# Score matmuls of 128 keys issued as four matmuls of 32 keys, one to each column group of TensorE

## The chip, the cores and the metric

The kernel runs on one core of one Trainium2 chip. The metric is the device time of one execution in microseconds (us). Work is spread over TensorE (PE in the profile; PEld is its weight loading), VectorE (DVE), ScalarE (ACT), GpSimd (POOL) and the DMA queues that SyncE (SP) issues.

## The reference

The reference embeds 1,024 patch tokens and 77 text tokens for each of 8 batches (1,101 tokens of 64 features), adds a state-space layer, and then adds this attention block, which takes about two thirds of the time:

```python
sx = jnp.einsum('bsh,ndh->bnsd', x, hl_w) + hl_b[None, :, None, :]
q = jnp.einsum('bnsd,neod->bneso', sx, wq)          # 4 heads n, 4 experts e, 16 features
k = jnp.einsum('bnsd,nod->bnso', sx, wk)            # one key set per head, shared by its experts
v = jnp.einsum('bnsd,nod->bnso', sx, wv)
scores = jnp.einsum('bnesd,bntd->bnest', q, k) * d ** 0.5 + causal
att = jax.nn.softmax(scores, axis=-1)
qkv = jnp.einsum('bnest,bntd->bnesd', att, v)
...                                                 # gate over experts, layer norm, two 16x16 layers, gate over heads
```

So for each batch, head and expert there are 1,101 queries by 1,101 keys under a causal mask.

## The kernel before, in words

The program has three parts: the embedding with the state-space layer, `stage_ffn_bounded` (the attention, on which everything below bears), and `stage_ffn_exact`, a second form of the attention behind a flag that these inputs do not set.

In `stage_ffn_bounded` the tokens are padded to 9 tiles of 128. Queries `qop` and keys `kop` lie in SBUF as 97 rows (six bf16 part products of 16 features and one row for a bound) by tokens. A **score matmul** (`scores`, L1923 to L1936) loads 128 keys of 97 rows as weights and streams up to 512 queries of one expert past them; in the last query tile, of 77 queries, one matmul streams the 77 queries of all four experts, 308 columns. Its result, 128 keys by queries, fills a PSUM bank of `pss`. `score_units` packs the pieces in banks and two banks in a unit: 23 units a head and 57 score matmuls a head (24 of 512 columns, 8 each of 384, 128 and 256, and 9 of 308). ScalarE takes the exponential of a unit (`b_pb<-b_pss`, L2051), GpSimd masks the diagonal blocks (L2089), and then the **value matmuls** (`sums`, L1938 to L1960) multiply the 32 columns of `vop` with the exponentials. The value matmul of expert e writes partitions 32e to 32e+31 of `pso`, so four of them, one per expert, stand in four column groups of the array. They are issued for 13 groups a head, each of one or two units, sorted so that the four experts of a key tile follow each other.

One batch is a period of 92 slots (4 heads of 23 units). In slot s TensorE issues the score matmuls of unit s, then, where a group is complete, the value matmuls of the units two slots back, then the **fillers** that the tables `PRO`, `EPI`, `ATT` and `RES` put in this slot: the projections of the next batch (L1918, L1995, L1998, L2003, L2007, L2010, L2011), the mixer of the finished head (L1986) and the layers behind the attention of the batch before (L1918, L2015, L2020). TensorE takes them strictly in this order. `scores` waits until the exponential two units back has been taken (`exped`), in the first unit of a head until the head's operands have landed (`placed`); `sums` waits for `exped` and `masked`.

`periods` (L1819) runs a first half period without attention, one period written out for batch 0, a loop whose body is run six times for batches 1 to 6, and two more written out. At the end of a body TensorE jumps back to its start. In slots 50 to 76 VectorE splits the next batch's queries and keys into bf16 parts (L2191 to L2196); SyncE stores them to DRAM (L1856 to L1867) and loads them back, head by head, in the layout of `qop` and `kop` (L1873, L1874, and the bound at L1878). The first unit of the next batch waits for head 0 of that.

Of the kernel before, what the change touches and what calls it, by code (L numbers as in the profile page):

```python
# [14 lines left out]
P = 128  # L15
# [78 lines left out]
NH, NE, HD = 4, 4, 16  # L94
# [1007 lines left out]
VW = 32  # L1102
# [578 lines left out]
def stage_ffn_bounded(nc, w, h2d, out, flag_d):  # L1681
# [15 lines left out]
    with ExitStack() as ctx:  # L1697
# [18 lines left out]
        qop = sb("b_qop", [KB_, NH, NE, LP], BF16)  # L1716
        kop = sb("b_kop", [KB_, NH, LP], BF16)
# [26 lines left out]
        pss = ps("b_pss", [P, 2, UB, QT])  # L1744
# [86 lines left out]
        with nc.Block() as block:  # L1831
# [69 lines left out]
            def _(pe):  # L1901
# [21 lines left out]
                def scores(p, u):  # L1923

                    n, un = divmod(u, NU)
                    if un == 0:
                        pe.wait_ge(placed[n], (p + 1) * (13 * 16))
                    pe.wait_ge(exped, p * NUB + u + 1)
                    for b, bank in enumerate(units[un]):
                        for col, j, e, q0, w in bank:  # L1930
                            lhs = kop[:, n, j * P:(j + 1) * P]
                            if e is None:
                                mm = pe.matmul(pss[:, u % 2, b, 0:NE * w], lhs, qop[:, n, :, q0:q0 + w], start=True, stop=True, skip_group_check=True)  # L1933
                            else:
                                mm = pe.matmul(pss[:, u % 2, b, col:col + w], lhs, qop[:, n, e, q0:q0 + w], start=True, stop=True, skip_group_check=True)  # L1935
                    mm.then_inc(scored, 1)  # L1936

                def sums(p, u):  # L1938
# [84 lines left out]
                def run(p, att, pro, prev):  # L2023
                    k[0], first[0] = 0, parity(p)
                    at = jobs(att, pro, prev)
                    if att and not prev:
                        pe.wait_ge(late_ok, 5)
                    for s in range(SPAN):
                        if att:
                            scores(p, s)  # L2030

                        if s < LAG and prev:
                            sums(p - 1, SPAN - LAG + s)
                        elif s >= LAG and att:
                            sums(p, s - LAG)
                        for kind, c in at.get(s, ()):
                            fill(jobs_before(p), p, kind, c)
# [423 lines left out]
```

## Time and profile before

| | |
|---|---|
| Median of 3 runs | 1675.55 us (1671.19 to 1684.4) |
| Profiled execution, span | 1670.1 us (the profile gives no other time for it) |
| TensorE matmul busy | 1341.6 us, 80% of the span, 11,103 matmul records |
| TensorE weight load busy | 628.3 us, 11,103 records |
| VectorE, ScalarE, GpSimd busy | 881.8, 775.4, 419.2 us |
| Mean granted TensorE clock | 0.845 of 2.4 GHz |

How to read it: times in the rows are microseconds from the start of the span, unless they are marked ns or are the mean of one instruction, which is in ns. An fp32 matmul of the program leaves two load records and two matmul records, a bf16 one leaves one of each. The record of a matmul covers its whole passage; the next may start long before its end, so what a matmul costs in a stream is the step from start to start. "issue" is time in which the engine waited for nothing that the profile shows.

### The profile page before, as it was taken

To read this page: it belongs to the slowest core of one execution; us is meant where nothing else is said; L and a number is where in the kernel's file an instruction comes from. 1 tells how busy PE (TensorE), PEld (TensorE's weight loads), DVE (VectorE), ACT (ScalarE), POOL (GpSimd) and SP (SyncE) were. 2 spreads that over 40 slices of the span, in tenths; PEclk is the share of its full clock that TensorE was granted. 3 is DMA by queue.
4 is the path that set the end of the run, shared out by engine and by line. 5 is a ranking of instruction groups with operands and counts; after the bars stand their busy time and mean duration, and the time that the engine had idled before them with its cause. 6 is when DMAs were issued, how large, how long until landed. Compare 5 with 4: busy or idle time off the path is not lost.

```text
span 1670.1 us, 32129 instructions
## 1 busy us (share of the span) xinstructions
PE 1341.6 (80%) x11103; PEld 628.3 (38%) x11103; DVE 881.8 (53%) x1824; ACT 775.4 (46%) x906; POOL 419.2 (25%) x619
## 2 busy tenths in 40 slices
PE   5888388915499899978988997899789979998942
PEld 3454287712154334323433432343234334333421
DVE  4667833275545544744673464538345735852343
ACT  0231244310256564556555455645564655675730
POOL 2000400053122241323323132423133232323421
PEclk9998699655599987889997888979797989998975
DMA  8995698031630360063036004500720270072000
GB/s 149 186 239 78 121 196 162 1 80 23 124 49 12 81 100 1 12 128 62 12 79 110 1 12 104 85 1 12 143 46 12 66 123 1 12 140 41 2 14 8
DMA packets 121421, 118.09 MB, mean 71 GB/s; under 512 B 73848, under 2 KB 90503, under 8 KB 121109
## 3 DMA queue, kind: packets, MB, share of 16 engines
q1 hardware_dynamic: 117216, 115.41, 36.1%
q8 instruction: 98, 1.61, 0.5%
q10 hardware_dynamic: 3733, 0.60, 0.3%
q14 instruction: 54, 0.44, 0.1%
q0 software_dynamic: 320, 0.04, 0.0%
HBM read 88.17 MB, written 22.95 MB: 67 GB/s over the span
## 4 chain that ended last, share of the span: by engine, by line
PE 41%; DVE 15%; issue 7%; DMA 5%; POOL 4%; SPq 3%; ACT 2%; DVEq 0%; POOLq 0%; ACTq 0%
PE b_pso L1959 13%; PE b_pss L1935 12%; POOL b_stat L2070 3%; PE b_psm L1986 3%; DMA qk_parts_b<-b_qs 3%; PE b_psm L2015 3%; ACT b_pb L2051 2%; PE b_psm L2003 2%; DMA b_qop<-bound_part 2%; PE b_psm L1918 2%; DVE b_rq L2193 2%; PE b_psm L1998 2%; PE b_psm L1995 1%; DVE b_qs L2191 1%; PE b_psm L2020 1%
## 5 line engine op out<-in xcount | busy, mean ns | idle before, releaser
L2051 ACT ACTIVATE b_pb<-b_pss 128x1024 f32<-128x1024 f32 (+2 forms) x736 | 667.7, 937 | 559.8 <-PE b_pss L1935 459.2
L2089 POOL TENSOR_SCALAR_AFFINE_SELECT b_pb<-b_pb 128x256 f32<-128x256 f32 (+1 forms) x544 | 230.4, 441 | 822.8 <-ACT b_pb L2051 816.8
L1959 PE MATMUL b_pso<-b_pb,b_vop 128*32 128x77 f32 (+4 forms) x5376 | 405.3, 414 | 27.1 <-POOL b_pb L2089 25.3
L1935 PE MATMUL b_pss<-b_qop,b_kop 97*128 97x512 bf16 (+3 forms) x1536 | 368.9, 357 | 67.7 <-issue 59.4
L1935 PEld LDWEIGHTS b_pss<-b_qop,b_kop 97*128 97x128 bf16 x1536 | 125.7, 106 | 295.2 <-issue 137.7
L1959 PEld LDWEIGHTS b_pso<-b_pb,b_vop 128*32 128x32 f32 x5376 | 118.2, 117 | 220.7 <-issue 138.4
L2278 DVE TENSOR_TENSOR b_ofm<-b_pso,b_mk 128x512 f32<-128x512 f32 (+1 forms) x96 | 51.6, 538 | 199.6 <-PE b_pso L1959 196.8
L2070 POOL TENSOR_TENSOR b_stat<-b_stat,b_mh 128x18 f32<-128x18 f32 x34 | 108.9, 3220 | 38.8 <-DVE b_stat L2349 27.3
L915 PE MATMUL psc<-tz,ub 128*64 128x128 f32 x1152 | 79.9, 283 | 44.7 <-DVE tz L1036 36.1
L2156 DVE COPY b_ot<-b_psm 128x336 f32<-128x336 f32 (+1 forms) x96 | 40.2, 418 | 133.9 <-PE b_psm L1986 132.8
L1986 PEld LDWEIGHTS b_psm<-w_mixer,b_ofm 128*128 128x128 f32 (+1 forms) x576 | 74.9, 200 | 75.2 <-issue 52.8
L1986 PE MATMUL b_psm<-w_mixer,b_ofm 128*128 128x84 f32 (+1 forms) x576 | 90.8, 298 | 1.1 <-DVE b_ofm L2278 0.3
L915 PEld LDWEIGHTS psc<-tz,ub 128*64 128x64 f32 x1152 | 71.8, 141 | 52.6 <-DVE ub L1032 33.7
L2003 PE MATMUL b_psm<-b_xt,w_all 65*128 65x384 f32 (+1 forms) x144 | 71.0, 584 | 11.3 <-DVE b_rq L2193 11.0
L396 PE MATMUL psy<-x,g 128*128 128x512 f32 x128 | 64.3, 660 | 8.5 <-DMA x<-in_x 5.3
L1933 PE MATMUL b_pss<-b_qop,b_kop 97*128 97x308 bf16 x288 | 64.1, 305 | 0.0
L1036 DVE COPY tz<-tz 64x1152 f32<-64x1152 f32 x40 | 29.7, 753 | 46.5 <-DMA tz<-taps 46.3
L956 ACT COPY tz<-tz 64x1152 f32<-64x1152 f32 x24 | 27.6, 1151 | 57.2 <-DMA tz<-taps 57.2
L1007 POOL TENSOR_TENSOR stat<-stat,mh 128x18 f32<-128x18 f32 x4 | 16.1, 4033 | 132.8 <-DVE stat L1066 132.8
L1918 PE MATMUL b_psm<-w_ident,b_xn 128*64 128x128 f32 x72 | 12.8, 293 | 43.3 <-DVE b_xn L2321 43.3
L396 PEld LDWEIGHTS psy<-x,g 128*128 128x128 f32 x128 | 26.4, 213 | 39.8 <-issue 30.8
L997 POOL MEMSET mh<- 128x18 f32 x1 | 0.1, 118 | 161.0 <-POOLq L252 161.0
(378 smaller groups left out, 1539.1 us busy)
## 6 DMA issues: line engine op xcount, KB each, us to landing
b_qop<-qk_parts_b SPq DMA_DIRECT2D x192, 144.0 KB
tz<-taps SPq DMA_DIRECT2D x64, 304.0 KB, 9.6
x<-in_x SPq DMA_DIRECT2D x16, 1024.0 KB, 13.5
qk_parts_b<-b_qs SPq DMA_DIRECT2D x16, 864.0 KB, 5.2
b_kop<-qk_parts_b SPq DMA_DIRECT2D x192, 36.0 KB
b_mk<-b_mskf SPq DMA_DIRECT2D x128, 36.0 KB, 4.1
qk_parts_b<-b_ks SPq DMA_DIRECT2D x8, 432.0 KB, 3.9
n_late<-id_d SPq DMA_DIRECT2D x1, 2400.0 KB, 9.4
```

Source lines behind the costliest of these rows:

```text
L396: mm = pe.matmul(psy[:, j, :], g[:, r], x[:, b % 3, 8 * j:8 * j + 8, r * V:(r + 1) * V], start=(r == 0), stop=(r == KB - 1))
L915: pe.matmul(psc[D * half:D * half + D, g, c, :], ub[:, g, c, o:o + D], taps_at(dl), start=(dl in (0, 2)), stop=(dl == 7), skip_group_check ...
L1933: mm = pe.matmul(pss[:, u % 2, b, 0:NE * w], lhs, qop[:, n, :, q0:q0 + w], start=True, stop=True, skip_group_check=True)
L1935: mm = pe.matmul(pss[:, u % 2, b, col:col + w], lhs, qop[:, n, e, q0:q0 + w], start=True, stop=True, skip_group_check=True)
L1959: mm = pe.matmul(pso[VW * ee:VW * (ee + 1), (3 * n + x) % 2, q0 - QT * x:q0 - QT * x + w], vop[0:r, j, n, :], pb[0:r, slot_, b, cc:cc + w] ...
L1986: mm = pe.matmul(bank()[0:wd, (a - c[0]) * MIXW:(a - c[0] + 1) * MIXW], ofm[:, (3 * n + x) % 2, (a - c[0]) * P:(a - c[0]) * P + wd], mixer ...
L2003: mm = pe.matmul(bank()[0:m, 0:FB], wall[:, g * P:g * P + m], xt[:, x * FB:(x + 1) * FB], start=True, stop=True)
L2015: mm = pe.matmul(bank()[0:D, 0:FB], fcw[:, i, :], (hx1 if i else fxt)[:, c * FB:(c + 1) * FB], start=True, stop=True)
L2051: nc.scalar.activation(pb[:, s % PB, 0:nb, 0:w], pss[:, s % 2, 0:nb, 0:w], ACT.Exp, scale=float(HD) ** 0.5).then_inc(exped, 1)
L2070: pool.tensor_tensor(st[:, 3, lo:hi], st[:, 2, lo:hi], mh[:, lo:hi], ALU.pow).then_inc(rstd, 1)
L2089: ins = pool.affine_select(out=v_, in_=v_, compare_op=ALU.is_ge, fill=0.0, base=0, pattern=pat, channel_multiplier=-1)
L2278: tt(ofm[:, (3 * n + x) % 2, 0:w], pso[:, (3 * n + x) % 2, 0:w], mk[:, n, QT * x:QT * x + w], ALU.mult).then_inc(acc_free, 1)
```

## The change

Each score matmul is replaced by four, whose weights are 32 of the 128 keys and whose results go to the 32 matching partitions of the same columns of `pss`. Each of the four streams the same queries. What is computed, the banks, the semaphores and the order of units, value matmuls and fillers stay. `VW` is 32 and `P` is 128. The exact form behind the flag is not changed.

```diff
                     for b, bank in enumerate(units[un]):
                         for col, j, e, q0, w in bank:
-                            lhs = kop[:, n, j * P:(j + 1) * P]
-                            if e is None:
-                                mm = pe.matmul(pss[:, u % 2, b, 0:NE * w], lhs, qop[:, n, :, q0:q0 + w], start=True, stop=True, skip_group_check=True)
-                            else:
-                                mm = pe.matmul(pss[:, u % 2, b, col:col + w], lhs, qop[:, n, e, q0:q0 + w], start=True, stop=True, skip_group_check=True)
+                            for g in range(P // VW):
+                                lhs = kop[:, n, j * P + VW * g:j * P + VW * g + VW]
+                                if e is None:
+                                    mm = pe.matmul(pss[VW * g:VW * g + VW, u % 2, b, 0:NE * w], lhs, qop[:, n, :, q0:q0 + w], start=True, stop=True, skip_group_check=True)
+                                else:
+                                    mm = pe.matmul(pss[VW * g:VW * g + VW, u % 2, b, col:col + w], lhs, qop[:, n, e, q0:q0 + w], start=True, stop=True, skip_group_check=True)
                     mm.then_inc(scored, 1)
```

The order of TensorE's instructions at three places follows. Sizes are output partitions by columns. The first place is the start of the loop's body, behind the jump; REGISTER_ALU and ISA are register work of the waits. Before:

```order
L1819 UNCONDITIONAL_BRANCH
L1819 ISA
L1928 ISA
L1935 MATMUL b_pss<-b_qop,b_kop 128x512 x2
L1946 ISA
L1959 MATMUL b_pso<-b_pb,b_vop 32x77 x16
```

Now:

```order
L1819 UNCONDITIONAL_BRANCH
L1819 ISA
L1928 ISA
L1936 MATMUL b_pss<-b_qop,b_kop 32x512 x8
L1947 ISA
L1960 MATMUL b_pso<-b_pb,b_vop 32x77 x16
```

Two score matmuls have become eight; what stands before and behind them has not moved. In the written-out period ahead of the loop, and in each body, 228 score matmuls become 912.

The second place is in the middle of the body, where scores (`b_pss`) and values (`b_pso`) alternate with no filler between. Before:

```order
L1935 MATMUL b_pss<-b_qop,b_kop 128x512 x2
L1959 MATMUL b_pso<-b_pb,b_vop 32x512 x4
L1928 REGISTER_ALU
L1935 MATMUL b_pss<-b_qop,b_kop 128x512 x2
L1928 REGISTER_ALU
```

Now:

```order
L1936 MATMUL b_pss<-b_qop,b_kop 32x512 x8
L1960 MATMUL b_pso<-b_pb,b_vop 32x512 x4
L1928 REGISTER_ALU
L1936 MATMUL b_pss<-b_qop,b_kop 32x512 x8
L1928 REGISTER_ALU
```

All of these now have 32 output partitions; before, two widths alternated.

The third place is a filler between two units' scores (L1918, a transposition by the identity). Before:

```order
L1935 MATMUL b_pss<-b_qop,b_kop 128x256 x4
L1912 REGISTER_ALU
L1918 MATMUL b_psm<-w_ident,b_fx 64x128
L1928 REGISTER_ALU
L1935 MATMUL b_pss<-b_qop,b_kop 128x512 x2
```

Now:

```order
L1936 MATMUL b_pss<-b_qop,b_kop 32x256 x16
L1912 REGISTER_ALU
L1918 MATMUL b_psm<-w_ident,b_fx 64x128
L1928 REGISTER_ALU
L1936 MATMUL b_pss<-b_qop,b_kop 32x512 x8
```

The filler is the same instruction at the same place, now between matmuls of 32 output partitions.

## Rows read from the trace of the kernel before

**Rows 1.** The page: span, TensorE's busy time, and the span in 40 slices.
```profile
span 1670.1 us, 32129 instructions
PE 1341.6 (80%) x11103; PEld 628.3 (38%) x11103; DVE 881.8 (53%) x1824; ACT 775.4 (46%) x906; POOL 419.2 (25%) x619
PEclk9998699655599987889997888979797989998975
```

**Rows 2.** The page: the chain that ended last, by engine.
```profile
PE 41%; DVE 15%; issue 7%; DMA 5%; POOL 4%; SPq 3%; ACT 2%; DVEq 0%; POOLq 0%; ACTq 0%
```

**Rows 3.** The chain from 873 to 1029 us: start, us, what.
```profile
869.65 4.81 DMA b_qop<-bound_part
...
896.89 1.03 ACT b_pb L2051
...
976.95 1.00 PE b_pso L1959 x8
...
990.63 0.72 DVE b_qs L2196
...
1013.43 7.11 DMA qk_parts_b<-b_qs
...
1026.74 4.83 DMA b_qop<-bound_part
```

**Rows 4.** Groups by form: count, then busy us, mean ns, idle before.
```profile
L1935 PE MATMUL b_pss<-b_qop,b_kop 97*128 97x512 bf16 x768 | 238.8, 405 | 66.0 <-issue 59.4 <-DMA b_qop<-bound_part 5.5
L1935 PEld LDWEIGHTS b_pss<-b_qop,b_kop 97*128 97x128 bf16 x1536 | 125.7, 106 | 295.2 <-issue 137.7 <-ACT b_pb L2051 129.8 <-DMA b_qop<-bound_part 2.1
```

**Rows 5.** Timeline, TensorE, 909 to 911 us: start, us, group, count.
```profile
909.38 0.59 PE L1935 MATMUL b_pss<-b_qop,b_kop 97*128 97x512 bf16 x2
...
909.59 0.38 PE L1935 MATMUL b_pss<-b_qop,b_kop 97*128 97x512 bf16 x1
909.90 0.74 PE L1959 MATMUL b_pso<-b_pb,b_vop 128*32 128x77 f32 x32
...
910.39 0.25 PE L1959 MATMUL b_pso<-b_pb,b_vop 128*32 128x77 f32 x4
910.57 0.60 PE L1935 MATMUL b_pss<-b_qop,b_kop 97*128 97x512 bf16 x2
```

**Rows 6.** Timeline, TensorE: four score pieces between transpositions; mixer, then scores.
```profile
914.78 1.06 PE L1935 MATMUL b_pss<-b_qop,b_kop 97*128 97x384 bf16 x4
915.63 1.06 PE L1918 MATMUL b_psm<-w_ident,b_fx 128*64 128x128 f32 x4
...
909.13 0.28 PE L1986 MATMUL b_psm<-w_mixer,b_ofm 128*128 128x84 f32 x1
909.24 0.30 PE L1933 MATMUL b_pss<-b_qop,b_kop 97*128 97x308 bf16 x1
```

**Rows 7.** Timeline, TensorE: first score matmuls of batches 1 to 7.
```profile
584.16 0.60 PE L1935 MATMUL b_pss<-b_qop,b_kop 97*128 97x512 bf16 x2 [3.65 <-DMA b_qop<-bound_part]
...
739.09 0.61 PE L1935 MATMUL b_pss<-b_qop,b_kop 97*128 97x512 bf16 x1 [2.91 <-issue]
...
877.78 0.61 PE L1935 MATMUL b_pss<-b_qop,b_kop 97*128 97x512 bf16 x1 [4.76 <-issue]
882.13 0.61 PE L1935 MATMUL b_pss<-b_qop,b_kop 97*128 97x512 bf16 x1 [3.75 <-issue]
...
1038.21 0.61 PE L1935 MATMUL b_pss<-b_qop,b_kop 97*128 97x512 bf16 x1 [3.00 <-issue]
...
1193.97 0.61 PE L1935 MATMUL b_pss<-b_qop,b_kop 97*128 97x512 bf16 x1 [3.47 <-issue]
...
1346.67 0.61 PE L1935 MATMUL b_pss<-b_qop,b_kop 97*128 97x512 bf16 x1 [2.91 <-issue]
...
1482.37 0.60 PE L1935 MATMUL b_pss<-b_qop,b_kop 97*128 97x512 bf16 x2 [1.82 <-DMA b_qop<-bound_part]
```

**Rows 8.** The page: the queue that fetches most instructions: packets, MB, share of 16 engines.
```profile
q8 instruction: 98, 1.61, 0.5%
```

## The prediction

> **What bounds the kernel now.** The busy shares come first [rows 1]: TensorE is at 80%, nothing else is near, so the kernel looks bound by TensorE. The chain of waits corrects that [rows 2]: only 41% of the span lies in its matmuls. So I read the chain over one batch in the loop, 873 to 1029 us [rows 3]; the other batches repeat it. It has three stretches. From about 883 to 980 us TensorE leads, with single pieces of ScalarE, GpSimd and VectorE between. From 980 to 1013 us the chain is VectorE's splitting of the next queries and keys. From 1013 us to the first scores of the next batch at 1034.60 it is the store of these parts (7.11 us), SyncE's issues, and the load of head 0 (4.83 us). A faster TensorE helps only in the first stretch, 97 of 156 us, and behind the load if TensorE is late there.
>
> It is late there. In five of the seven later batches the first score matmul stands alone, and the second comes after 2.91, 3.75, 3.00, 3.47 and 2.91 us in which TensorE waited for nothing shown [rows 7]. These are the five batches that TensorE reaches by the jump back to the loop's start. The two that it reaches without a jump, at 584.16 and 1482.37 us, have both matmuls in 0.60 us. So behind the jump the instructions run out after the first few, and the next piece of the program has to be fetched. The fetching queue moved 98 packets of 16.4 KB (1.61 MB) [rows 8]; 22,206 loads and matmuls came in them [rows 1], with register work besides, so a packet holds some 230 to 260 instructions. The loop's start lies a handful of instructions ahead of a packet's end.
>
> What the change touches is the step between matmuls. Two score matmuls of 512 columns start 0.21 us apart (909.38 and 909.59), which is 512 columns at 2.4 GHz [rows 5]: loads are hidden, and the streaming is all. The value matmuls show what four column groups do: four of 77 columns, with their four loads, step by 0.07 us in all (32 records from 909.90, the last four from 910.39), and each streams 77 columns twice, so the four stream together and at full rate.
>
> Where one kind follows the other there is a gap. The last score matmul starts at 909.59 and is streamed by 909.80; the first value matmul starts at 909.90. The last four value matmuls (910.39) are streamed by 910.47; scores start at 910.57 [rows 5]. A switch costs 0.095 us, either way. A transposition between scores costs nothing of the kind: four score pieces of 1024 columns take 0.85 us from start to start of what follows (914.78 to 915.63), their bare streaming at 1.2 GHz [rows 6]. The mixer's 128-wide weights cost little (909.13 to 909.24, 0.11 us for 84 columns that stream in some 0.08). So the gap goes with the width of the column groups, not with the operands.
>
> **The change, part by part.**
>
> Streaming itself: four matmuls of 32 keys together for one of 128. By the value matmuls' step this is equal, 0.21 us for 512 columns. Zero for the stream; only the last of the four starts later, by what I put at a quarter of the 0.07 step, 0.02 us. That delays ScalarE where it leads, some ten places a batch: 7 x 10 x 0.02 = 1.4, rounded up to +2 us. A piece of 128 columns streams in 0.053 us, and four loads must fit in that; the nearest row is four loads in 0.07 us. Bounds 0 and 256 such pieces x 0.017 = 4 us; I take 0, since the 0.07 there is the streaming.
>
> A rule speaks against this. The Trainium skill (TensorEngine Tiling (Array Packing), Restrictions and Gotchas) says that column tiling switches fast weight load off, and its page TensorE: Matmul & The Clock Gate (LDWEIGHTS) has a load cost its columns over 1.2 GHz, 27 ns for 32, so 107 ns for four if they queue. By that the short pieces would add up to 256 x 0.054 = 14 us. The value loads of rows 5, four in 70 ns, speak against the queueing.
>
> Switches: in the order of the loop's body there are 128 changes of width before and 78 after. 85 vanish (52 from scores to values, 24 back, 9 at norm fillers of 16 columns) and 35 are new (around transpositions and 128-wide fillers, which now have scores of 32 on one or both sides). In the stretch that TensorE leads 45 vanish and 23 are new, 7 of them behind the mixer. 45 x 0.095 = 4.3; 16 x 0.095 + 7 x 0.055 = 1.9; 2.4 us a body, 14 for six. Some of these gaps lie beside a piece of ScalarE's (1.03 us at 896.89 [rows 3]) and are worth nothing, so -12. In the stretches of VectorE and the store they are worth nothing: what covers them is that chain. Batch 0 is written out and full of transpositions: 79 vanish, 59 are new, +7.5 - 5.3, taken as -1.5. Batch 7 has no next batch to prepare and is led by TensorE with ScalarE and GpSimd: 87 vanish, 19 new, 7.0 us, two thirds taken, -4.5.
>
> The way to the jump: from 1013 to 1029 us TensorE works beside the store and load, then jumps, and its first score starts 3 us after the load has landed (1031.57 to 1034.60). It waits for code there, so reaching the jump sooner counts: some 6 switches less, 5 x 0.6 = -3.
>
> The second wait behind the jump: each of the 684 added matmuls in batch 0's period brings a load, 1,368 instructions ahead of the loop's start, which moves against the packets' edges. If the edge is far enough, the next packet comes while TensorE works. The five idle times sum to 16.0 us, and the second matmul would step by 0.21 instead of standing behind 0.61: 5 x 0.40 more, 18 us. Bounds: 0 (the edge again right behind the start) and -18. A full wait needs the edge within the first slot's twenty of some 240 instructions; a partial one within about half. I take -15.
>
> By the Trainium skill (Runtime: NRT & Kernel Launch, Instruction fetch mechanics) a packet is 256 instructions, the next is fetched while one runs, and a jump breaks this. By it 1,368 is five packets and 88, the start stands about 83 into a packet with 173 ahead, and the term would be -18.
>
> Sum: +2 - 12 - 1.5 - 4.5 - 3 - 15 = **-34 us**. The profiled execution's span is 1670.1, so 1636 for it; the median is 5.4 above that span and the lowest run 1.1 (1671.19), as runs scatter. Against the median: 1675.55 - 34 = 1642.
>
> **Rivals.**
>
> *The wait behind the jump stays, or a like one appears* (packets rise from about 12 a body by 1,368/240 = 5.7, so fetching is more frequent; but in the densest stretch, 909.38 to 910.57 [rows 5], there would be some 80, so that a packet still lasts 3.6 us, a little more than the waits of rows 7). For it: one edge position is as good as another. Only the switches count: -19 to -22, 1655.
>
> *The gap is not of the width*, but of something that stays between scores and values. Then no switch goes, none comes: -15 + 2, 1662. Against it stand the transpositions and mixer of rows 6.
>
> *The four groups don't stream together* for bf16, one column per cycle each. This is the side on which it gets slower. All score matmuls have 678,528 columns, 768 x 512 [rows 4] and the shorter ones, 278 us by the step of 0.21. TensorE leads 97 of 156 us, so each 10% on the step costs 17 us, and from 20% on (0.25 us for 512 columns) the change loses. Two at a time, a doubled step, would give 1642 + 172 = 1814. Against it: the value matmuls stream four groups at that rate; but they are fp32, and no bf16 matmul of the trace is in four groups.
>
> The Trainium skill (TensorE: Matmul & The Clock Gate, Part 3) measured 2.38x for three column tiles of 512. If the missing fifth were streaming, the step would be 1.26 times as long: 1642 + 45 = 1687.
>
> *The clock moves.* It falls and rises within each batch [rows 1] after stretches with little or much work. TensorE's granted mean is 0.845; a shift of 0.03 either way over the led stretches (0.62 of the 1150 us that attention takes) is 25 us: 1617 or 1667. Nothing shows a sign, so it widens the range.
>
> **How the numbers follow.** Forecast 0.48 (1642); wait stays 0.22 (1655); gap not of the width 0.07 (1662); groups not together 0.11 (1687 and up); clock 0.12, half each way. A measurement of this kernel tells 1% (17 us) from no change, so faster means below 1659. Faster: nearly all of the first, two thirds of the second, a third of the third, half of the clock's, 0.69; slower: nearly all of the fourth, whose prices begin at 1687, 0.10; within 1%: 0.21. The range, 1618 to 1672, takes in the first three and the clock, and leaves out the groups.
>
> **What the profile after would show.** Eight score matmuls where two stood, stepping by 0.21 us per four; if that is 0.25 or more, the forecast is wrong. From scores to values a step without the 0.095, and a new 0.095 on both sides of transpositions. Behind each of the five jumps a first unit without idle time between its matmuls; the first score still 2 to 3 us after the load. VectorE's 33 us and the store's 7 us unchanged. A clock line that differs by more than 0.02 in the mean would make the sum unsafe.

## The result, and the profile after

The changed kernel takes 1620.49 us in the median of 4 executions (1615.22 to 1626.38); beside it on the same chip the kernel before took 1679.97 (1671.19 to 1691.62). The ratio is 0.9624, 95% interval 0.9562 to 0.9687: 59 us less, where the forecast was 34 less. In the two profiled executions the spans differ by 45.5 us, since the one of before [rows 1] is the quickest of its four and the one of the changed kernel (1626.38) the slowest of its four.

Executions of one kernel scatter with the clock that they are granted (54 of the kernel before: from 1651 us at 0.859 to 1701 us at 0.830), so the times of runs below are medians over all executions, quick and slow, with the granted clock beside them, and only ratios and intervals are of the quick ones alone.

The page of the changed kernel, the lines that answer to [rows 1, 2, 8]:

```profile
span 1624.6 us, 43073 instructions
PE 1297.7 (80%) x16575; PEld 675.3 (42%) x16575; DVE 878.8 (54%) x1824; ACT 771.2 (47%) x906; POOL 421.1 (26%) x619
PEclk9999699755589998899799979879997998999975
PE 38%; DVE 17%; issue 6%; DMA 5%; POOL 5%; SPq 3%; ACT 3%; DVEq 0%; POOLq 0%; ACTq 0%
q8 instruction: 134, 2.20, 0.7%
```

TensorE's share of the chain fell from 41 to 38%, by some 67 us (the shares are rounded to whole per cent), though its records of matmuls are 5,472 more. The other engines' busy times are within 1% of what they were. The mean granted clock is 0.863 instead of 0.845.

Its timeline of TensorE from 905 to 909 us answers to [rows 5, 6]; columns: start us, us, engine, line, group, count.

```profile
904.80 0.62 PE L1936 MATMUL b_pss<-b_qop,b_kop 97*32 97x256 bf16 x16
905.35 0.30 PE L1918 MATMUL b_psm<-w_ident,b_fx 128*64 128x128 f32 x1
905.58 0.62 PE L1936 MATMUL b_pss<-b_qop,b_kop 97*32 97x512 bf16 x8
906.02 1.04 PE L1960 MATMUL b_pso<-b_pb,b_vop 128*32 128x384 f32 x16
906.89 0.61 PE L1936 MATMUL b_pss<-b_qop,b_kop 97*32 97x512 bf16 x8
907.48 0.64 PE L1960 MATMUL b_pso<-b_pb,b_vop 128*32 128x256 f32 x8
```

From 905.58 to 906.02 lie eight score matmuls of 512 columns and the switch to the values: 0.44 us, where two times 512 columns at 2.4 GHz are 0.43. So four of 32 keys step by 0.21 like one of 128, and the gap of 0.095 is gone. The sixteen of 256 columns from 904.80 are streamed by 905.23 (four times 256 columns at 2.4 GHz are 0.43); the transposition starts at 905.35. There the new gap stands, 0.12 us.

The first score matmuls of batches 1 to 7, which answer to [rows 7], from the timeline of the changed kernel (in brackets the idle time before):

```profile
579.69 1.04 PE L1936 MATMUL b_pss<-b_qop,b_kop 97*32 97x512 bf16 x8 [2.41 <-DMA b_qop<-bound_part]
726.17 1.04 PE L1936 MATMUL b_pss<-b_qop,b_kop 97*32 97x512 bf16 x8 [4.28 <-DMA b_qop<-bound_part]
869.44 1.04 PE L1936 MATMUL b_pss<-b_qop,b_kop 97*32 97x512 bf16 x8 [4.37 <-issue]
1013.12 1.04 PE L1936 MATMUL b_pss<-b_qop,b_kop 97*32 97x512 bf16 x8 [4.76 <-issue]
1159.07 0.76 PE L1936 MATMUL b_pss<-b_qop,b_kop 97*32 97x512 bf16 x8 [3.70 <-DMA b_qop<-bound_part]
1302.84 1.04 PE L1936 MATMUL b_pss<-b_qop,b_kop 97*32 97x512 bf16 x8 [4.00 <-DMA b_qop<-bound_part]
1444.93 0.62 PE L1936 MATMUL b_pss<-b_qop,b_kop 97*32 97x512 bf16 x8 [3.17 <-DMA b_qop<-bound_part]
```

All eight of a unit stand together in every batch; the wait of 2.91 to 3.75 us between the first and the rest is gone.

Where the rest went shows when batch 3 is cut at the same exponentials in both traces. Columns: stretch, its length, busy us of PE, PEld, DVE, ACT and POOL, then the granted clock, DMA share and GB/s. Of the kernel before, from the first exponential of slot 0 to that of slot 12, of 35 to 46, and of 46 to 58:

```profile
882.80:898.90 16.10, 15.96 (x132) 5.82 (x135) 7.82 (x21) 11.92 (x14) 3.11 (x8) 0.81 0.70 113
934.80:957.40 22.60, 21.36 (x170) 12.08 (x166) 10.41 (x19) 9.09 (x12) 3.60 (x9) 0.85 0.00 1
957.40:983.20 25.80, 25.80 (x145) 7.81 (x149) 12.36 (x30) 12.02 (x12) 9.60 (x10) 0.67 0.00 1
```

The same three of the changed kernel:

```profile
870.50:885.00 14.50, 13.46 (x222) 6.28 (x218) 7.88 (x21) 11.56 (x14) 3.12 (x8) 0.92 0.73 129
918.40:940.90 22.50, 21.39 (x255) 12.61 (x255) 10.46 (x19) 9.25 (x13) 3.61 (x9) 0.85 0.01 1
940.90:962.90 22.00, 22.00 (x235) 8.01 (x231) 12.06 (x30) 12.03 (x12) 9.61 (x10) 0.77 0.01 2
```

Where the clock is the same, the length is (22.60 and 22.50). Where TensorE held 2.4 GHz longer (0.67 to 0.77) it is 3.8 us shorter, and the busy times of the other engines are nearly unchanged. Batch 3, from its first exponential to that of batch 4, takes 156.1 us before and 143.7 after. Of the 12.4 us, 7.7 lie in three stretches whose clock rose (the first and the last of those shown, and slots 23 to 35, 0.79 to 0.92), 4.1 at the jump, 0.6 in all the rest.

### The profile page after: what moved, and what is told of

Read it like the earlier page. It is cut to its first block, busy times and chain, and to the rows that moved or that the text cites. A ratio compares the mean times of both kernels' runs of the same rounds, so it can differ in the third digit from the quotient of the medians.

```text
span 1624.6 us, 43073 instructions
## 1 busy us (share of the span) xinstructions
PE 1297.7 (80%) x16575; PEld 675.3 (42%) x16575; DVE 878.8 (54%) x1824; ACT 771.2 (47%) x906; POOL 421.1 (26%) x619
## 4 chain that ended last, share of the span: by engine, by line
PE 38%; DVE 17%; issue 6%; DMA 5%; POOL 5%; SPq 3%; ACT 3%; DVEq 0%; POOLq 0%; ACTq 0%
PE b_pss L1936 11%; PE b_pso L1960 11%; POOL b_stat L2071 4%; DMA qk_parts_b<-b_qs 3%; PE b_psm L1987 3%; ACT b_pb L2052 3%; PE b_psm L2016 3%; PE b_psm L1918 2%; PE b_psm L2004 2%; DVE b_rq L2194 2%; PE b_psm L1999 2%; DMA b_qop<-bound_part 2%; DVE b_qs L2192 2%; DVE b_qs L2197 2%; PE b_psm L1996 2%
## 5 line engine op out<-in xcount | busy, mean ns | idle before, releaser
L1960 PE MATMUL b_pso<-b_pb,b_vop 128*32 128x77 f32 (+4 forms) x5376 | 394.6, 404 | 34.3 <-POOL b_pb L2090 32.8
L1936 PE MATMUL b_pss<-b_qop,b_kop 97*32 97x512 bf16 (+3 forms) x6144 | 375.2, 353 | 54.2 <-issue 26.1
L1936 PEld LDWEIGHTS b_pss<-b_qop,b_kop 97*32 97x32 bf16 x6144 | 131.8, 100 | 264.3 <-ACT b_pb L2052 123.2
L1960 PEld LDWEIGHTS b_pso<-b_pb,b_vop 128*32 128x32 f32 x5376 | 149.6, 121 | 152.8 <-issue 53.2
L1934 PE MATMUL b_pss<-b_qop,b_kop 97*32 97x308 bf16 x1152 | 70.1, 307 | 0.0
L1918 PE MATMUL b_psm<-w_ident,b_xn 128*64 128x128 f32 x72 | 13.1, 298 | 43.4 <-DVE b_xn L2322 43.4
```

The costliest lines, as they stand in the source:

```text
L1934: mm = pe.matmul(pss[VW * g:VW * g + VW, u % 2, b, 0:NE * w], lhs, qop[:, n, :, q0:q0 + w], start=True, stop=True, skip_group_check=True)
L1936: mm = pe.matmul(pss[VW * g:VW * g + VW, u % 2, b, col:col + w], lhs, qop[:, n, e, q0:q0 + w], start=True, stop=True, skip_group_check=True)
L1960: mm = pe.matmul(pso[VW * ee:VW * (ee + 1), (3 * n + x) % 2, q0 - QT * x:q0 - QT * x + w], vop[0:r, j, n, :], pb[0:r, slot_, b, cc:cc + w] ...
```

## The experiments

Two groups of causes are to be told apart. In the forecast's sum were the switches and the wait behind the jump. Not in it was the clock. A slot below is one of the 92 of a batch. "Written out" means that TensorE's loop over batches is replaced by all periods one after the other, so that it never jumps:

```diff
-                periods(pe, run)
+                for p in range(-1, B + 1):
+                    run(p, 0 <= p < B, p < B - 1, p > 0)
```

### The wait behind the jump

88 instructions that only count a semaphore up, ahead of TensorE's attention, push the loop's start of the kernel before along; 168 do the same to the changed kernel, back towards a packet's end.

```diff
+                for _ in range(88):          # e2: 168, in the changed kernel
+                    pe.sem_inc(passed, 1)
                 pe.wait_ge(const_ok, 1)
```

> The kernel before, with 88 semaphore increments that nobody waits for put at the start of TensorE's part of the attention, where TensorE waits for the first tokens anyway: no matmul is added or moved, only the loop's start moves by 88 instructions against the edges of the fetched packets, as the 1,368 instructions of the change do. Theory (the second wait behind the jump is an edge right behind the loop's start): the two first score matmuls of each body stand together, 3 to 3.5 us less at each of five jumps, 16 to 20 us less in all, ratio 0.988 to 0.991 of before. Rival (the wait belongs to something else, such as the queue's load or the operands): nothing changes, ratio 1.00.

> The changed kernel with 168 such increments, which put the loop's start back to where it was against the edges before. Edge theory: a second wait of about 3 us returns behind the first score matmul or its four at each of five jumps, 16 to 20 us more than the changed kernel's 1620, ratio to before 0.972 to 0.978. If narrower score matmuls were the reason that the wait is gone, it stays gone: 0.962.

e1 took 1658.28 us (1647.81 to 1674.09) beside 1683.18 of the kernel before (1653.77 to 1694.57): 25 less, without any change in a matmul. e2 took 1652.01 (1645.6 to 1655.38), 31 more than the changed kernel took beside its own partner. The timeline of e1 behind its jump into batch 3:

```profile
873.76 1.03 PE L1937 MATMUL b_pss<-b_qop,b_kop 97*128 97x512 bf16 x2 [4.55 <-issue]
```

and of e2 behind the jump into batch 2:

```profile
734.41 0.38 PE L1938 MATMUL b_pss<-b_qop,b_kop 97*32 97x512 bf16 x1 [3.62 <-issue]
737.58 1.04 PE L1938 MATMUL b_pss<-b_qop,b_kop 97*32 97x512 bf16 x7 [2.79 <-issue]
```

The padding alone takes the second wait from the kernel before and gives it to the changed one: one matmul alone, 2.79 us, then seven. So it belongs to where the loop's start lies in a packet. By the waits of [rows 7] it is 2.91 to 3.75 us for each of five jumps, 16 in sum. From the last exponential of a batch to the first of the next the five crossings take 48.0 us before and 28.8 in e1, 26.0 in the changed kernel and 46.1 in e2: 19 less and 20 more, in the profiled executions. The times of e1 and e2 differ by more than that, and by more than the 16 to 20 that was expected of each; the rest goes with the clock, as far as is seen: its median is 0.845 in e1 where the kernel before has 0.839 over all its executions, and 0.859 in e2 where the changed kernel has 0.866.

### Without a jump

> The kernel before with TensorE's six bodies written out instead of looped, the other engines as they are: no jump for TensorE, so no fetch behind one. Edge theory: both waits at the five batch boundaries go, about 7 us each as at the boundary that had no jump (2.4 us from the last exponential of a batch to the first of the next, against 9 to 10), 30 to 36 us less, ratio about 0.98. Rival (the load of head 0 ends the wait whatever TensorE does): 16 to 20 us less.

> The changed kernel with TensorE's bodies written out. With no jump in either, its distance to the kernel before written out is what the width of the scores gives by itself: by the sum of the prediction 12 + 1.5 + 4.5 - 2 = 16 us, 1.0%. If the part of the gain that the prediction lacks (the changed kernel gained some 60 us, not 34) comes from the clock or the switches, the distance is 30 us or more; if it came from the jumps, it is 16 us or less.

e3: 1643.09 us (1613.49 to 1646.29), clock 0.851; that is 40 less than its partner, where 30 to 36 was expected. e4: 1597.47 (1593.17 to 1604.55), clock 0.873. Without any jump the two forms still stand 46 us apart. The forecast had put 16 us on the switches. The slots 46 to 58 of batch 3, with the columns as above, in e3:

```profile
942.40:968.20 25.80, 25.80 (x146) 7.85 (x149) 12.39 (x30) 12.05 (x12) 9.53 (x10) 0.67 0.00 1
```

and in e4:

```profile
929.40:951.50 22.10, 22.10 (x235) 8.07 (x231) 12.13 (x30) 12.11 (x13) 9.60 (x10) 0.77 0.01 1
```

Same lengths and same clocks as in the two kernels with the loop: what differs in this stretch does not come from the jump.

The low level comes in pieces. In the middle of a batch stands the longest; here it is in the kernel before and e3, then in the changed kernel and e4, with the columns as above:

```profile
950.40:974.30 23.90, 23.56 (x146) 9.66 (x145) 9.24 (x23) 7.25 (x8) 6.42 (x10) 0.50 0.00 1
935.30:959.20 23.90, 23.56 (x146) 9.81 (x145) 9.24 (x23) 7.25 (x8) 6.28 (x10) 0.50 0.00 1
934.10:951.20 17.10, 16.88 (x162) 8.21 (x162) 6.65 (x17) 5.21 (x6) 2.58 (x7) 0.50 0.00 1
922.70:939.80 17.10, 16.88 (x163) 8.21 (x161) 6.65 (x17) 5.21 (x6) 2.67 (x7) 0.50 0.01 2
```

In batches 1 to 6 of the traces of before, e1 and e3 this piece is 23.9 us in eleven batches, 17.1 in four and absent in three; in those of the changed kernel, e2 and e4 it is 17.1 in seventeen and absent in one, never 23.9. So the low level does not come in the middle of each batch, as the text ahead of e5 has it.

Where it is absent, slots 46 to 58 run at 2.4 GHz throughout, and the form of the scores can be compared at the same clock. Batch 2 of the kernel before, and batch 1 of e8, which is e4 again:

```profile
809.20:827.30 18.10, 18.10 (x145) 6.09 (x143) 12.47 (x30) 12.04 (x13) 9.61 (x10) 1.00 0.00 1
647.60:664.80 17.20, 17.20 (x231) 6.83 (x225) 11.89 (x30) 12.04 (x12) 9.61 (x10) 1.00 0.01 2
```

The switches are worth 0.9 us there, and the clock 5 to 8.

### Where in the batch

If the clock in slots 35 to 58 carries the rest, scores of 32 keys there alone should bring it, and scores of 128 there alone should lose it. Both written out:

```diff
-                def scores(p, u):
+                def scores(p, u, width=VW):
...
-                            for g in range(P // VW):
-                                lhs = kop[:, n, j * P + VW * g:j * P + VW * g + VW]
+                            for g in range(0, P, width):
+                                lhs = kop[:, n, j * P + g:j * P + g + width]
...
-                            scores(p, s)
+                            scores(p, s, VW if 35 <= s < 59 else P)      # e6: P if 35 <= s < 59 else VW
```

> TensorE's bodies written out; only the scores of slots 35 to 58 of each batch are issued as four of 32 keys, all others as one of 128. In these slots the granted clock falls to its lower level in each batch of all four traces so far. Clock theory (the narrow scores save only about 2 us a batch at equal clock, and the rest of the distance between the two kernels written out, 46 us, is that TensorE, packed more densely behind the fall, is granted the upper level again sooner): most of the distance stands already here, slots 46 to 77 take some 36 us of each batch as in the changed kernel, against 39 to 42 before, and the time is 1605 to 1625. Rival (the gain is spread over all switches alike): about a quarter of the distance, 1630 to 1635.

> The reverse: slots 35 to 58 issue one matmul of 128 keys, all other slots four of 32. Clock theory: slots 46 to 57 take 25 to 26 us as before, and 69 to 77 16 us, and the time is 1615 to 1630. Rival (spread alike): about three quarters of the distance, 1608 or less.

e5: 1616.47 us (1588.22 to 1621.16), clock 0.865. e6: 1628.28 (1614.05 to 1632.0), ratio 0.9704 (0.9606 to 0.9801), clock 0.861. Both lie between e3 and e4, in clock as in time, and both are in the range that the clock theory gave. Slots 46 to 58 take 21.8 us in the mean of batches 1 to 6 in e5 and 24.1 in e6, beside 25.0 in e3 and 22.1 in e4: in this stretch the time follows the form of the scores there. The middle of the batch carries more than its quarter of the slots, but neither part carries all. Four executions of each, which scatter by 18 to 33 us, give no closer shares.

### Two groups of 64 keys

The same function, called with `scores(p, s, 64)`, written out. Now there is a switch between scores and values again, and another towards the 128-wide fillers: 145 in the order of a body, more than the 128 of the kernel before.

> TensorE's bodies written out; each score matmul is two of 64 keys. If the gap belongs to a change of width between one instruction and the next, it stays at 0.095 us between scores and values, goes between scores and fillers of 64, and is new around those of 128: 145 switches a body against 128 before and 78 changed, so 1 to 2 us a batch more than before written out, 1645 to 1655. If any cut of the scores made the stream denser, it would lie between 1597 and 1643.

Measured: 1627.09 us (1623.11 to 1629.07), ratio 0.971 (0.9643 to 0.9778), clock 0.869. The count of switches had asked for 1645 to 1655 and missed. Its timeline:

```profile
909.36 0.62 PE L1936 MATMUL b_pss<-b_qop,b_kop 97*64 97x512 bf16 x4
909.91 1.07 PE L1960 MATMUL b_pso<-b_pb,b_vop 128*32 128x384 f32 x16
...
912.03 0.54 PE L2016 MATMUL b_psm<-b_fxt,w_fcw 65*64 65x384 f32 x1
912.04 0.62 PE L1936 MATMUL b_pss<-b_qop,b_kop 97*64 97x512 bf16 x2
912.40 0.49 PE L2016 MATMUL b_psm<-b_fxt,w_fcw 65*64 65x384 f32 x1
912.73 0.60 PE L1936 MATMUL b_pss<-b_qop,b_kop 97*64 97x512 bf16 x2
```

From 909.36, 0.43 us of streaming and then 0.12 to the values: the gap is there. But the score matmul at 912.04 starts 0.01 us behind the start of a filler pass that has 0.32 us to stream. Filler and scores of 64 columns each run side by side, as two column groups can. It saves the gap and little more: the other two score matmuls come behind the filler's second pass, at 912.73, and from 912.03 to the end of their streaming it is 1.13 us, where filler and scores one after the other stream for 1.07. So this does not explain 16 us less than e3; the higher clock does (0.869 to 0.851). An estimate parts the two: the time at 1.2 GHz is twice the missing share of the clock times the time of the execution, and over all executions of all these kernels each us of it goes with 0.41 us of time. Brought to the same 430 us at 1.2 GHz, e7 takes 1630 us and the 128-wide form of e3 1618. At an equal clock the 64-wide form is 12 us slower, which is what the count of switches had asked for (2 to 12 more), and what it missed is the clock.

### Fewer switches, more switches, denser streams

e8 is e4 again, as a partner. e9 gives each run of scores between two others the width that both neighbours have in common (128 beside transpositions, projections and the mixer, 64 beside the two layers), else 32; 55 switches a body instead of 78. e10 is e4 with a matmul of one column and 128 keys ahead of each unit's scores, which puts two switches into every unit; its result is overwritten.

```diff
                     pe.wait_ge(exped, p * NUB + u + 1)
+                    pe.matmul(pss[:, u % 2, 0, 0:1], kop[:, n, 0:P], qop[:, n, 0, 0:1], start=True, stop=True, skip_group_check=True)
```

> The changed kernel with TensorE's bodies written out once more, as the neighbour on the same chip of the next two: 1597 as before, ratio 0.94 to 0.955 of the kernel before.

> Written out, and the scores of each unit in the width that its two neighbours have where both have the same (128 between transpositions, mixer or 128-wide projections, 64 between the 64-wide layers), else in 32: by the order 55 switches a batch instead of 78. Switch theory: 23 x 0.1 us, two thirds of them where TensorE leads, 1.5 us a batch, 8 to 12 us less than the narrow kernel written out, 1585 to 1590. Clock theory adds that fewer gaps bring the upper level back no later, so not more time at the lower level than 22 us a batch.

> The narrow kernel written out, with a matmul of one column and 128-wide weights ahead of each unit's scores (its result is overwritten by them): two more switches for nearly each of the 92 units, so more gaps than the kernel before has, but the same narrow score matmuls. If the clock comes back sooner because the stream is denser, the time at the lower level rises from 22 us a batch to 34 or more as in the kernel before, and the time goes to 1660 or more (92 x 0.2 us x 0.6 x 7 = 77 us of gaps). If it comes back sooner because narrow matmuls count for more, the time at the lower level stays at 22 us and slots 46 to 57 keep a granted clock of 0.76 or more, and only the gaps are paid.

e8: 1599.64 us (1594.48 to 1609.83), ratio 0.9591 (0.9521 to 0.9662), clock 0.873. e9: 1590.0 (1570.55 to 1597.97), ratio 0.9459 (0.9363 to 0.9555), clock 0.872: 10 us less than e8 at the same clock, as expected from the switches. e10: 1612.75 (1603.62 to 1635.05), ratio 0.9628 (0.9513 to 0.9743), clock 0.887, in four executions. Its slots 46 to 58 of batch 3:

```profile
943.00:961.50 18.50, 18.50 (x243) 7.54 (x237) 12.37 (x30) 12.00 (x12) 9.60 (x10) 1.00 0.01 2
```

18.50 us at full clock, where e4 took 22.1 at 0.77 and e3 25.8 at 0.67. So it is in five of its batches 1 to 6; in batch 2 it takes 26.0 us at 0.68. At full clock that is 18.6, against 18.1 for 128 keys and 17.2 for 32 keys. The gaps are paid, as its timeline shows, 0.10 us from the one column to the scores and as much ahead of it:

```profile
950.37 0.18 PE L1929 MATMUL b_pss<-b_qop,b_kop 97*128 97x1 bf16 x1
950.48 0.61 PE L1937 MATMUL b_pss<-b_qop,b_kop 97*32 97x512 bf16 x8
950.92 1.04 PE L1961 MATMUL b_pso<-b_pb,b_vop 128*32 128x384 f32 x16
951.89 0.18 PE L1929 MATMUL b_pss<-b_qop,b_kop 97*128 97x1 bf16 x1
```

This felled my first theory of the clock, that narrow scores keep it up because the gaps are gone and the stream is denser: e10 puts gaps back, and its clock is the highest of all.

### What in the form of the scores holds the clock

Three kernels from e3, the 128-wide form written out, go for what is left: the one-column matmul as in e10 (e11, e15), the number of matmuls (e12, e14, the full score matmuls cut to 128 queries each: 153 a head instead of 57, each still one matmul of 128 keys), and e3 again (e13).

```diff
-                                mm = pe.matmul(pss[:, u % 2, b, col:col + w], lhs, qop[:, n, e, q0:q0 + w], start=True, stop=True, skip_group_check=True)
+                                for f in range(0, w, P):
+                                    mm = pe.matmul(pss[:, u % 2, b, col + f:col + f + P], lhs, qop[:, n, e, q0 + f:q0 + f + P], start=True, stop=True, skip_group_check=True)
```

> The kernel before, TensorE's bodies written out, with the same matmul of one column ahead of each unit's scores, which stay 128 wide: no switch is added, 644 matmuls are. The clock held up in the run with extra switches (16 us a batch at the lower level, against 22 with narrow scores alone and 34 with wide ones). If it is the narrow form of the scores that holds it up, this one stays at 30 us a batch or more and near 1643. If any small matmul more does, it falls to 25 us or less and the time to 1630 or less.

> The kernel before, written out, with each score matmul cut along the queries into pieces of 128, so about three times as many instructions, the same 128-wide weights loaded again for each, the same switches. If the number of matmuls and loads counts for the clock, the time at the lower level falls to some 22 us a batch as with the narrow scores, and the time to 1605 to 1630. If it is the narrow form (four column groups at once), it stays at 30 or more and 1643 to 1655.

> The kernel before, TensorE's bodies written out, once more and with more executions, as the neighbour on one chip of the next two. Mean granted clock over the run 0.850 to 0.853 in most executions, time about 1643, as in its first run (0.850, 0.850, 0.852, 0.872).

> The kernel with scores 128 wide and cut along the queries, once more. If the number of matmuls and loads raises the granted clock, its mean is again above the uncut kernel's in the same call by 0.010 or more (its first run had a median of 0.863). If only four groups at once do, the means agree within 0.005 and the first run was scatter.

> The kernel with scores 128 wide and a matmul of one column ahead of each unit, once more. Small matmuls count: mean granted clock again 0.010 or more above the uncut kernel's (0.866 in its first run). They don't: within 0.005.

Medians of each form over all executions of its runs, all with the loop written out; the last column is the estimate from above, the mean time brought to 430 us at 1.2 GHz:

| Scores | Executions | Clock | Median us | At 430 us of 1.2 GHz |
|---|---|---|---|---|
| 128 keys (e3, e13) | 10 | 0.851 | 1642 | 1618 |
| 128 keys, cut to 128 queries (e12, e14) | 11 | 0.858 | 1636 | 1620 |
| 128 keys, one-column matmul (e11, e15) | 10 | 0.865 | 1630 | 1626 |
| 32 keys (e4, e8) | 10 | 0.873 | 1598 | 1611 |
| 32 keys, one-column matmul (e10) | 4 | 0.887 | 1613 | 1639 |

e11 alone was 1627.51 us, e15 1629.78; e12 1622.93, e14 1636.76; e13 1639.63. A one-column matmul a unit lifts the clock by 0.014 with either width, and costs 8 us beside 128 keys and 28 beside 32 keys at an equal clock. Cutting the stream lifts it by 0.007, no more than single executions differ; e14 beside e13 on one chip gave 0.858 and 0.853, between its two expectations. Neither accounts for the 0.022 of four column groups.

### The best form, once more

If one column lifts the clock as such, then in the width of its scores, where it brings no switch, it should add to e9.

> The kernel with three widths, written out, once more as the neighbour of the next on one chip: 1590, mean granted clock 0.872.

> The same with a matmul of one column ahead of each unit's scores, in the width of these scores, so that no switch is added. One such matmul a unit went with a mean granted clock 0.014 higher over wide scores (0.865 against 0.851) and 0.014 higher over narrow ones (0.887 against 0.873). If that carries over, the clock is 0.885 and the time 10 to 15 us less, 1575 to 1580. If in the narrow case it came from the 128-wide form of the added matmul and its switches, the clock stays at 0.872 and the time at 1590 to 1595.

e16, which is e9: 1592.31 us (1582.32 to 1601.21), ratio 0.9562 (0.9485 to 0.964), clock 0.871. e17: 1599.06 (1588.58 to 1604.78), ratio 0.9614 (0.9529 to 0.9699), clock 0.875. Missed: 7 us more, and the clock rose by only 0.004; at an equal clock, by the same estimate, it is 12 us more. So one more one-column matmul does not lift the clock as such. By e10 and e17 alone one could put it on the change of width that comes with it; but in e11 and e15 it has the width of its scores, adds no change of width, and the clock is 0.014 higher. Three widths without it (e9, e16) is the best version found, about 29 us below the changed kernel: 23 of that come with the loop written out (e4), the rest with the widths.

## Why the forecast was right in kind and too small

**The stream at full rate: right.** Eight matmuls and a switch in 0.44 us at 905.58. The four loads hide even behind the shortest pieces: at 968.05 four matmuls of 128 columns are followed by the next after 0.056 us, as one of 128 keys is in the trace before. The Trainium skill's rule that column tiling switches fast weight load off (TensorEngine Tiling (Array Packing), Restrictions and Gotchas) would by the prediction's estimate have added 14 us, and the trace shows nothing of it. And the Trainium skill's 2.38x for three column tiles (TensorE: Matmul & The Clock Gate, Part 3) is not a limit for the four here, by the 0.44 us at 905.58.

**The switches: right in kind, a little high.** The gap goes with the change of width, on both sides of a transposition as between scores and values. One count was off. The key norm filler has 16 columns, so I let its switches vanish; it has 64 rows, and the timeline after shows 0.1 us on both sides of it still:

```profile
961.36 0.60 PE L1936 MATMUL b_pss<-b_qop,b_kop 97*32 97x512 bf16 x8
961.89 0.33 PE L2008 MATMUL b_psm<-b_squares,w_blkkb 64*16 64x384 bf16 x1
962.15 0.62 PE L1936 MATMUL b_pss<-b_qop,b_kop 97*32 97x512 bf16 x8
```

(961.36 and 0.43 of stream is 961.79, the filler starts at 961.89; with its 0.16 it ends at 962.05, the scores start at 962.15.) So 79 switches vanish, not 85. That it is the rows shows the query norm, of 16 columns too but of 128 rows: the scores start 0.09 us behind its start, before its 0.16 are streamed.

```profile
991.46 0.33 PE L2011 MATMUL b_psm<-b_squares,w_blkqb 128*16 128x384 bf16 x1 [0.27 <-DVE b_rq L2194]
991.55 0.40 PE L1936 MATMUL b_pss<-b_qop,b_kop 97*32 97x512 bf16 x3
```

In the trace before, where the scores have 128 keys, the fillers of L2003, of 65 rows and 128 columns, have no gap to them (0.003 us), and those of L2020, of 64 rows and 128 columns, have 0.14. The gap is one of rows and columns together.

Worth: straight lines through the ten executions of each written-out form, time over granted clock, give 1621 and 1614 us for 128 keys at 0.865 and 0.870, and 1609 and 1604 for 32 keys, 10 to 12 less. Only two executions of 128 keys came that high; the estimate at an equal time at 1.2 GHz gives 7. Forecast for the same was 12 + 1.5 + 4.5 - 2 = 16. The gaps are as priced, 0.095 us, so too many of them were taken to count.

**The wait behind the jump: right,** in place, cause and size. Taken as 15, with 18 as the bound; it is five times 2.9 to 3.75, 16 in sum, gone in the changed kernel as in e1. With the 3 us for the way to the jump the forecast had 18 at the five crossings; by the exponentials they take 22 less (48.0 and 26.0). By the Trainium skill's packet of 256 instructions (Runtime: NRT & Kernel Launch, Instruction fetch mechanics) I had given the loop's start 173 instructions ahead; the change moved it by 1,368, five packets and 88, and with 168 more (e2), six whole packets from where it was, the wait is back; 88 alone (e1) puts the kernel before where the changed one stands. So the runs agree with that length. The first score matmul still comes behind the load, though by less than the 2 to 3 us of the list: in batch 4 the load lands at 1011.61, and it starts at 1013.12. The chain of waits of the changed kernel:

```profile
993.25 7.10 DMA qk_parts_b<-b_qs
...
1007.33 4.28 DMA b_qop<-bound_part
```

**VectorE and the store: right.** The store of the parts takes 7.10 us, VectorE's busy time 878.8.

**The clock: the step that failed.** The forecast said of it, "Nothing shows a sign, so it widens the range", gave it a chance of 0.12, and put it at nothing in the sum. It has a sign. With the loop written out nothing but the form differs, and over ten executions each the clock is 0.851 and 0.873, the time 1642 and 1598; e3 and e4 alone, on one chip, show the same clocks. Of these 44 us 7 to 12 are there at equal clock; the other 32 to 37 come with the clock. Over batches 1 to 6 of the profiled executions the time of a batch, from the start of its first exponential to that of its last, follows the time that TensorE spends at 1.2 GHz closely: it is 128.8 us plus 0.42 of it with 128 keys (before, e1, e3, 18 batches) and 129.3 plus 0.36 with 32 keys (after, e2, e4, 18 batches), with a mean of 33.3 us a batch at 1.2 GHz in the one and 23.6 in the other. So nearly ten us less at the low level a batch, at 0.4 each, is 4 us a batch and 27 in seven.

Put together, as an estimate, for the measured 59: 7 to 12 for the switches, 16 to 22 for the wait and the way to the jump, and about 30 for the clock (27 by the batches above, 32 to 37 by the written-out forms). The forecast had the first two at 34. The last line of its list (a mean clock that differs by more than 0.02 would make the sum unsafe) is what came: 0.866 over the executions of the changed kernel to 0.839 over all of the kernel before, though only 0.863 to 0.845 in the two that were profiled.

**The rivals.** Wait stays, gap not of the width, and groups not together fell with the rows above. "The clock moves" was right, upward, and not instead of the forecast but on top of it; that it was listed as a case beside the others and not as a term that adds to each of them is why the range ended too high: the ratio 0.9624 on the 1675.55 us that the forecast started from is 1613, below its lower end of 1618. That the rival's 1617 lies near the measured 1620 is in part luck, since its 25 us were a shift of 0.03 picked for either way.

**What stays open.** Why the scores' form moves the granted clock. Shown is that denser streaming isn't it (e10 has more gaps and a higher clock), that cutting the stream in shorter matmuls brings a third at most (e12, e14), and that a one-column matmul a unit brings 0.014 in 128 columns, beside scores of 128 (e11, e15) and of 32 keys (e10), and 0.004 in the width of its scores where these have three widths (e17). A common reading, that changes in the width of what TensorE works on hold the clock, fits e10 and e17, but not e11 and e15, which add none, nor e9, which has 23 fewer a body than e8 at the same clock, nor that the changed kernel has fewer such changes than the kernel before and a higher clock. Whether a matmul of 32 output columns counts for less than one of 128, whatever runs beside it, was not tested by itself: a kernel with four column groups that are given the same columns one after the other, so not overlapping, was not tried.

## What to carry to other kernels

Where a matmul of full width stands between matmuls in column groups, give it their width if it has enough columns to stream: here the rate was the same and each change of width saved was 0.1 us on TensorE; beside a full-width neighbour on both sides leave it wide. Before adding up such gains look at the granted clock by stretch: if TensorE drops to 1.2 GHz for a fifth of a batch, the form of the matmuls may be worth more through the clock than through the gaps, and a forecast has to carry that as a term on top of each case. And a loop's start behind a jump is worth a look: the same body was 25 us quicker, 19 of them at the five jumps, when 88 empty instructions stood ahead of it.

## What the runs showed of the hardware that was not expected

- The granted clock went with the form of the matmuls at equal work: 0.851 with scores in one matmul over all columns and 0.873 with four of 32 columns, 0.887 with these and a one-column matmul of full width a unit (e10, four executions).
- In e10, 736 one-column matmuls and the two gaps at each cost only 13 to 15 us in all, because the clock was higher: the stretch from slot 46 to 58 ran in 18.6 us instead of 22 in five of six batches. At an equal clock they are put at 28.
- An fp32 matmul of 64 columns and bf16 matmuls of 64 stream side by side (e7, 0.01 us between their starts), while towards the values of 32 the gap remains, 0.12 us. The pair saves its gap and little more.
- A change of the rows that a matmul uses, 97 to 64, costs the same 0.1 us as a change of columns; 97 to 65 and 97 to 128 cost nothing.
- From the last exponential of a batch to the first of the next the changed kernel takes 4.4 to 5.8 us over a jump and 3.5 and 3.8 without one, the written-out e3 and e4 1.6 to 3.3, and the kernel before, whose loop starts right ahead of a packet's end, 9.2 to 10.0.
